# A four-layer graph network on one core: norm and projection in one stage, batch norm in blocks, part tables on ScalarE, scatter landings waited for later

## The reference, cut to what matters

```
deg_isqrt = max(segment_sum(1, dst), 1) ** -0.5
x = layernorm(x + gat_gat(x))                 # layer 0: two attention convolutions, relu between
x = layernorm(x + conv_conv_conv(x))          # layer 1: 3x elu(segment_sum(x[src]) @ W_rel + b + x @ W_root)
x = layernorm(x + batch_layer(x, deg_isqrt))  # layer 2
x = layernorm(x + attention(x, edge_attr))    # layer 3

attention: h = x @ W (4 heads of 64), a_src = h . att_src, a_dst = h . att_dst per head
           e = leaky_relu(a_src[src] + a_dst[dst]); softmax of e over the edges of each dst
           out[dst] += h[src] * softmax (times edge_attr in layer 3)
batch_layer: y = segment_sum(edge_weight * x[src]) + eps_weight * x
             h = relu(batchnorm(y @ w1.T));  y = (h @ w2.T) * deg_isqrt
             return relu(batchnorm(y)) + x      # batch norm: mean and variance over the nodes
```

## Time and profile before

| what | value |
|---|---|
| time, median of 3 runs | 8349.84 us (8339.62 to 8362.3) |
| the profiled execution's own time | 8344.37 us |
| its span in the trace | 8342.6 us |
| PE busy | 4909.4 us, 59% of the span |
| VectorE busy | 3812.1 us, 46% |
| ScalarE busy | 1028.3 us, 12% |
| POOL busy | 5501.9 us, 66% |
| granted clock of TensorE, mean | 0.783 of full speed |

### The profile page before, as it was taken

The page is one execution under the profiler, slowest core; times in us unless marked ns, Lnnn a source line. Parts: engine busy times, 40 slices in busy tenths (PEclk is TensorE's granted clock), DMA queues, the critical chain, the costliest instruction groups (busy, mean ns, idle before and its releaser), DMA issues. The chain is left out here.

```text
span 8342.6 us, 83489 instructions
## 1 busy us (share of the span) xinstructions
PE 4909.4 (59%) x17596; PEld 3782.0 (45%) x17597; DVE 3812.1 (46%) x6764; ACT 1028.3 (12%) x2857; POOL 5501.9 (66%) x5858
## 2 busy tenths in 40 slices
PE   4455565555562666666666666666566666455554
PEld 3344444344452554555545555455444453344443
DVE  5566665566665222242222422225222236566666
ACT  2000003000003000020000200003333323000003
POOL 5777754777733777757777577775777750777770
PEclk7677777787786887888877888788677787777776
DMA  5444433444424443344433444334333334444441
GB/s 177 133 119 117 117 84 109 118 119 117 117 60 151 133 132 105 105 139 133 134 105 105 136 133 135 106 105 145 109 105 105 105 96 134 130 119 119 119 118 65
DMA packets 499012, 982.41 MB, mean 118 GB/s; under 512 B 121598, under 2 KB 303930, under 8 KB 498177
## 3 DMA queue, kind: packets, MB, share of 16 engines
q0 software_dynamic: 274784, 746.53, 32.0%
q1 hardware_dynamic: 155901, 176.58, 6.7%
q10 hardware_dynamic: 68080, 56.84, 2.1%
HBM read 889.06 MB, written 97.65 MB: 118 GB/s over the span
## 5 line engine op out<-in xcount | busy, mean ns | idle before, releaser
L1578 POOL DMA_INDIRECT l1aa_messages<-table,l1aa_index x784 | 741.1, 945 | 465.0 <-issue 238.5
L1578 POOL DMA_INDIRECT l2a_messages<-table,l2a_index x784 | 741.2, 945 | 259.0 <-issue 238.5
L1578 POOL DMA_INDIRECT l1ca_messages<-table,l1ca_index x784 | 741.2, 945 | 249.4 <-issue 238.5
L1578 POOL DMA_INDIRECT l1ba_messages<-table,l1ba_index x784 | 741.2, 945 | 248.9 <-issue 238.5
L1205 POOL DMA_INDIRECT l3a_messages<-table_h,l3a_index x782 | 745.1, 953 | 238.2 <-issue 237.0
L1205 POOL DMA_INDIRECT l0aa_messages<-table_h,l0aa_index x782 | 743.4, 951 | 238.2 <-issue 238.2
L1205 POOL DMA_INDIRECT l0ba_messages<-table_h,l0ba_index x782 | 743.2, 950 | 238.2 <-issue 238.2
L1742 PE MATMUL l1aa_sums<-l1aa_messages,l1aa_member 128*128 x1952 | 584.4, 461 | 457.1 <-SPq L1587 449.4
L1742 PE MATMUL l2a_sums<-l2a_messages,l2a_member 128*128 x1952 | 612.5, 484 | 400.5 <-ACT l2a_messages L1626 396.7
L1742 PE MATMUL l1ba_sums<-l1ba_messages,l1ba_member 128*128 x1952 | 584.6, 462 | 364.0 <-SPq L1587 359.5
L1742 PE MATMUL l1ca_sums<-l1ca_messages,l1ca_member 128*128 x1952 | 585.3, 462 | 362.1 <-SPq L1587 358.2
(11 more groups left out here) (649 smaller groups left out, 6998.7 us busy)
## 6 DMA issues: line engine op xcount, KB each, us to landing
table<-l_acc SPq DMA_DIRECT2D x10, 1280.0 KB
l2b_xin<-table SPq DMA_DIRECT2D x100, 128.0 KB, 2.0
l1aa_messages<-table,l1aa_index POOLq DMA_INDIRECT x784, 2.8
l1ba_messages<-table,l1ba_index POOLq DMA_INDIRECT x784, 2.7
l1ca_messages<-table,l1ca_index POOLq DMA_INDIRECT x784, 2.8
l2a_messages<-table,l2a_index POOLq DMA_INDIRECT x784, 2.7
l0aa_messages<-table_h,l0aa_index POOLq DMA_INDIRECT x782, 3.0
l0ba_messages<-table_h,l0ba_index POOLq DMA_INDIRECT x782, 2.9
```

Source lines behind the costliest of these rows:

```text
L1578: pool.indirect_dma_start(out=ring4[:, g % ROUND, j, 0:D], out_offset=None, in_=table, in_offset=bass.IndirectOffsetOnAxis(ap=index[:, g * ...
```

## The change

It has five parts.

1. `started` becomes a semaphore of the whole program, `k.started`, which is never cleared. The waits for it at the end of the prelude, of l0e and of the projection before layer 3 are gone. The attend phase gets an argument `starts` (1, 2 or 3), and SP issues index, same and local, then waits for `starts * 16 * NT`, and only then loads `start_dram`.
2. In the prelude the order on TensorE becomes project(17, 25), turn_place(1), turn_at(1), project(25, 35), local table of the sums, project(35, 50), local table of attention.
3. In the joins 24 activations of ScalarE (Copy with `of_pair`'s column as scale) make the member tables, four of them ahead of the exponential; TensorE waits for each part's table as it comes to it.
4. l2b: the first stage goes by blocks of four tiles. The product with w1 is made for 512 columns at once, ScalarE copies it to `zT`, VectorE takes statistics of 512 columns, and only 13 of them are aggregated. In the last stage the relu runs in place on `zT` by blocks, and TensorE turns `zT` directly. The slots of x are eight, the loops are written out, the four columns are loaded from ScalarE's queue, TensorE begins on the weights alone, and n_norm is stored and loaded after the load of tile 16.
5. l2n and l3p become one phase `norm_project_phase`, named l3p. ScalarE norms each tile in `acc` (Identity with scale and bias), TensorE turns it from there, nothing is loaded again. The normed table is stored in ten stores of 640 KB that stand between the stores of h on SP. `h_out` has eight slots and `h_ps` four.

```diff
-            pool.wait_ge(started, 16 * NT)
...
-            project(17, 22)
+            project(17, 25)
             turn_place(1)
             turn_at(1)
-            project(22, 30)
+            project(25, 35)
             step_local_on_tensor(pe, k, ws, wide[2])
-            project(30, NTP)
+            project(35, NTP)
             step_local_on_tensor(pe, k, wa, wide[2])
...
-            sp.dma_start(start, start_dram[0:ELEM].rearrange("(r e) h -> r (e h)", e=RL)).then_inc(starts_in, 16)
             sp.dma_start(same, same_dram).then_inc(starts_in, 16)
             sp.dma_start(local[:], steps.local_dram).then_inc(local_in, 16)
+            sp.wait_ge(k.started, starts * 16 * NT)
+            sp.dma_start(start, start_dram[0:ELEM].rearrange("(r e) h -> r (e h)", e=RL)).then_inc(starts_in, 16)
...
+            def members(a, b):
+                for n in range(a, b):
+                    act.activation(member[W, n, :], one_hot[W], ACT.Copy, scale=of_pair[W, n:n + 1]).then_inc(member_made, 1)
+
+            act.wait_ge(hot_made, 1)
+            members(0, 4)
             act.wait_ge(less_made, 1)
             act.activation(weight[W], weight[W], ACT.Exp).then_inc(weight_made, 1)
+            members(4, NCUT)
 
...
-            pe.wait_ge(member_made, 1)
+            pe.wait_ge(parts_made, 1)
             for n in range(NCUT):
+                pe.wait_ge(member_made, n + 1)
...
-            st(dve.tensor_tensor(member[W], repeat_outer(one_hot[W], NCUT), repeat_inner(of_pair[W], P), ALU.mult))
...
+            def store_x(n):
+                sp.wait_ge(normed, (n + 1) * LOAD)
+                rows = table_out[n * LOAD * P:(n + 1) * LOAD * P, :].rearrange("(t p) d -> p t d", p=P)
+                sp.dma_start(rows, acc3[:, n * LOAD:(n + 1) * LOAD, 0:D]).then_inc(x_stored, 16)
+
+            for t in range(NTP):
+                if t % LOAD == 0:
+                    store_x(t // LOAD)
+                sp.wait_ge(h_made, t + 1)
+                sp.dma_start(table_h[t * P:(t + 1) * P, :], h_out[:, t % 8, :]).then_inc(stored[t % 8], 16)
...
+            act.wait_ge(norm_ready, 1)
+            for i in range(NTP + BEHIND):
+                if i < NTP:
+                    here = acc3[:, i, 0:D]
+                    act.activation(here, here, ACT.Identity, scale=var[:, i:i + 1], bias=mean[:, i:i + 1]).then_inc(normed, 1)
+                t = i - BEHIND
+                if t >= 0:
+                    act.wait_ge(turned, t + 1)
+                    if t >= 2:
+                        act.wait_ge(summed, t - 1)
+                    act.copy(xt[:, t % 2, :], xt_ps[t % 2][:, 0:D]).then_inc(xt_made, 1)
+
+        @block.tensor
+        def _(pe):
+            def turn(t):
+                pe.wait_ge(normed, t + 1)
+                if t >= 2:
+                    pe.wait_ge(xt_made, t - 1)
+                for c in range(2):
+                    at = t * MSGW + c * P
+                    ins = pe.transpose(xt_ps[t % 2][:, c * P:(c + 1) * P], acc[:, at:at + P], k.ident[:])
+                ins.then_inc(turned, 1)
+
+            def multiply(t):
+                pe.wait_ge(xt_made, t + 1)
+                if t >= 4:
+                    pe.wait_ge(h_made, t - 3)
+                for c in range(2):
+                    ins = pe.matmul(h_ps[t % 4][:, 0:WE], xt[:, t % 2, c * P:(c + 1) * P], w_sb[:, c, :],
+                                    start=(c == 0), stop=(c == 1))
+                ins.then_inc(summed, 1)
+
...
+            dve.sem_inc(norm_ready, 1)
+            dve.wait_ge(w_in, 64)
+            weights_with_scores(dve, st, w_sb, att, prod)
+            dve.sem_inc(w_ready, 1)
+            for t in range(NTP):
+                dve.wait_ge(summed, t + 1)
+                if t >= 8:
+                    dve.wait_ge(stored[t % 8], t // 8 * 16)
+                dve.tensor_copy(k.att[:, t * 2 * H:(t + 1) * 2 * H], h_ps[t % 4][:, D:WE])
+                dve.tensor_copy(h_out[:, t % 8, :], h_ps[t % 4][:, 0:WE]).then_inc(h_made, 1)
...
+            sp.dma_start(eps_w[:], eps_weight.partition_broadcast(P)).then_inc(eps_in, 16)
+
+            def load(t, sem):
+                sp.dma_start(xin[:, t % SLOTS, :], table_in[t * P:(t + 1) * P, :]).then_inc(sem[t % SLOTS], 16)
+
+            for t in range(NTP):
+                if t >= SLOTS:
+                    sp.wait_ge(y_made, t - SLOTS + 1)
+                load(t, loaded)
+                if t == 2 * SLOTS:
+                    sp.wait_ge(degT_made, 1)
+                    sp.dma_start(norm_dram.rearrange("(t p) -> t p", p=P), degT[0:NTP, :]).then_inc(deg_stored, 16)
+                    sp.wait_ge(deg_stored, 16)
+                    sp.dma_start(n_norm[:], norm_dram.partition_broadcast(P)).then_inc(norm_in, 16)
+            for t in range(NTP):
+                if t < SLOTS:
+                    sp.wait_ge(y_made, t + (NTP - 1 - t) // SLOTS * SLOTS + 1)
...
-            pe.wait_ge(small_in, 144)
+            pe.wait_ge(w_in, 64)
...
+            def turn(t):
                 pe.wait_ge(y_made, t + 1)
+                if t >= 2:
                     pe.wait_ge(yT_made, t - 1)
                 for c in range(2):
+                    ins = pe.transpose(ps[4 + t % 2][:, c * P:(c + 1) * P], yin[:, t % 4, c * P:(c + 1) * P], k.ident[:])
                 ins.then_inc(turned, 1)
 
+            def multiply(n):
+                b, w = blocks[n]
+                pe.wait_ge(yT_made, (b + w) // P)
+                if n >= 2:
+                    pe.wait_ge(z_made, n - 1)
                 for o in range(2):
                     for c in range(2):
+                        ins = pe.matmul(ps[2 * (n % 2) + o][:, 0:w], wT[:, 0, c, o * P:(o + 1) * P],
+                                        yT[:, n % 2, c, 0:w], start=(c == 0), stop=(c == 1))
                 ins.then_inc(summed, 1)
 
+            for t in range(NTP):
+                turn(t)
+                if t >= 2 and (t - 2) % BT == BT - 1:
+                    multiply((t - 2) // BT)
+            multiply(len(blocks) - 1)
+            pe.wait_ge(z_made, len(blocks))
...
+            def take(t):
+                n, j = t // BT, t % BT
                 act.wait_ge(turned, t + 1)
+                if n >= 2:
+                    act.wait_ge(summed, n - 1)
+                act.copy(yT[:, n % 2, :, j * P:(j + 1) * P],
+                         ps[4 + t % 2][:, 0:D].rearrange("p (c n) -> p c n", c=2)).then_inc(yT_made, 1)
+
+            def keep(n):
+                b, w = blocks[n]
+                act.wait_ge(summed, n + 1)
+                for o in range(2):
+                    ins = act.copy(zT[:, o, b:b + w], ps[2 * (n % 2) + o][:, 0:w])
+                ins.then_inc(z_made, 1)
+
+            for t in range(NTP):
+                take(t)
+                if t >= 4 and (t - 4) % BT == BT - 1:
+                    keep((t - 4) // BT)
+            for n in range((NTP - 4) // BT, len(blocks)):
+                keep(n)
 
...
+            for b, w in blocks:
                 for o in range(2):
+                    ins = act.activation(zT[:, o, b:b + w], zT[:, o, b:b + w], ACT.Relu,
                                          bias=bias[:, o:o + 1], scale=scale[:, o:o + 1])
...
+            def add_own(t):
+                dve.wait_ge(loaded[t % SLOTS], (t // SLOTS + 1) * 16)
+                if t >= 4:
+                    dve.wait_ge(turned, t - 3)
+                dve.scalar_tensor_tensor(yin[:, t % 4, :], xin[:, t % SLOTS, :], eps_w[:], acc3[:, t, 0:D],
                                          op0=ALU.mult, op1=ALU.add).then_inc(y_made, 1)
 
+            def block_stat(n, stats):
+                b, w = blocks[n]
+                for o in range(2):
+                    dve.bn_stats(stats[:, o, n * 6:(n + 1) * 6], zT[:, o, b:min(b + w, N)]).then_inc(stats_made, 1)
+
+            for t in range(NTP):
+                add_own(t)
+                if t >= 7 and (t - 7) % BT == BT - 1:
+                    n = (t - 7) // BT
+                    dve.wait_ge(z_made, n + 1)
+                    block_stat(n, block_stats[0])
+            for n in range((NTP - 7) // BT, len(blocks)):
+                dve.wait_ge(z_made, n + 1)
+                block_stat(n, block_stats[0])
+            dve.wait_ge(stats_made, 2 * len(blocks))
+            dve.wait_ge(cols_in, 64)
```

330 lines of the change are left out of this document (96 added, 234 removed).

## The result

The changed kernel takes 8265.67 us (median of 4 runs, 8262.86 to 8277.6); the kernel before, on the same chip, 8347.40 (median of 4, 8339.62 to 8362.3). The ratio is 0.9907 with a 95% interval of 0.9895 to 0.9919, so 68 to 88 us faster. Predicted were 8268 and 8240 to 8304.

The account below looks back on a forecast made before the run. POOL's gathers fill the attend and sum phases and move as blocks, so only the chains between them gain: 3.0 + 7 + 8.7 + 21 + 37.6 = 77.3 off 8344.4 gives 8267, plus 1: 8268 us, range 8240 to 8304.

Parts of the forecast that it names:

- The reading of the chain: Whole kernel: gathers on POOL move as blocks; a microsecond saved in the chains between them is saved at the end.
- The start load behind the landing: Start of attend phases: the load comes at worst some 2 us later, within VectorE's slack; costed at nothing.
- Landing: Phase boundaries behind l0e and l3p: dropping the wait for scatters to land saves 1.5 us each, 3.0 together.
- rival B: Boundaries behind scatters: the silent microseconds all stay and the landing lies under them; 4.5 us less gain, 8273; chance 0.13.
- Prelude: End of the prelude: reordered projection ends 5 us earlier, the dropped landing wait saves 2; together 7.
- Joins: Three joins: member tables moved from VectorE to ScalarE save 2.9 us each, exponential 0.5 late; 8.7 together.
- l2b: Batch norm layer: start 2.5, first stage 8, aggregate 2, second stage -0.5, last stage 9; gain 21 us.
- Fused phase: Norm and projection as one, before layer 3: POOL's scatters pace it; gain 37.6 us, bounds 28 and 40.
- A: Boundaries behind scatters: the silent microseconds go with the wait, 11 us more gain, 8257; chance 0.14.
- C: l2b's first stage: PE runs dry behind VectorE's statistics, up to 34 us, or the n_norm load starves xin; 8302; chance 0.07.
- E: Attend tails: PE's clock falls to 0.50, costing 121 us in three tails; 8388, slower than before; chance 0.02.
- D: Fused phase: x stores between h stores on SP make VectorE wait for slots, 31 us; 8299; chance 0.07.

Follow-up runs that it names:

- gap_late: The changed kernel without the last 24 of l3p's 49 scatters, and with n_norm loaded after stage one's loads: 8261.5 us, ratio 0.9896 to the kernel before.
- again: The changed kernel run once more, unaltered, in another group of runs: 8269.2 us against 8348.5 for the kernel before, ratio 0.9906.
- p39_slots4: The changed kernel with four more tiles projected ahead of the prelude's local table and four h_out slots in the fused phase: 8264.8 us, ratio 0.9901.
- u_wait: The changed kernel with the landing waits back at the ends of the prelude, l0e and l3p, on a slow chip: 10432.7 us, ratio 0.9936.
- wait_again: The changed kernel with the same three landing waits back, on another slow chip: 10444.7 us, ratio 0.9919 to the kernel before.

## Why the prediction was right

- **The reading of the chain** held: gathers move as blocks, and what was saved between them arrived, but for the 3 to 4 us by which the prelude and l0e vary from trace to trace. The gains outside the gathers sum to 85 and 76 in two traces, and the times moved by 82 and 79; 77.3 were predicted. The start load behind the landing, costed at nothing, cost nothing: the first softmax step stands 46.5 to 47.5 behind the first gather in before and 46.9 to 47.6 in after.
- **Landing**: 1.5 taken at two boundaries and 2 at the prelude's, 1.3 to 1.9 measured at all three. The argument, that the silent part comes after all traffic and so isn't landing, is shown by the two wait runs, and gap_late shows whose it is. The Trainium skill's fixed cost of about 2.0 per DMA ("DMA: Bandwidth & Descriptors", "Anatomy of one DMA — SWDGE (gpsimd) path") gave the upper side of it. Two sums beside this term slipped: with 2 for the prelude, rival B is 5.0 less and not 4.5, and the page's price would add 1.0 and not 1.5.
- **Prelude**: 7 predicted, 6.5 measured in after (2.2 in again, late from before the edit), with the right size by luck. The prediction had PE's idle of 4.44 ahead of the local table shrink. On the quick chips it stayed (5.0), since VectorE has the table's operands some 16.5 us after the turn in either order; what counts is how many tiles are projected before it. Five more were, and 5 x 1.1 is the gain. What the edit did gain of idle time stood at the turn of places: 1.68 in before, none in after. That 5 us were still left ahead of the table was not seen, and p39_slots4 took them.
- **Joins**: 2.9 each predicted, 3.1 measured from the first turn to the first product; of this 2.3 and 2.8 arrive in the stretches of the last two joins, where the work behind the first product takes 0.4 to 0.5 longer. The half microsecond for a late exponential was not there; the activations take 0.30 and not 0.45 each. The Trainium skill's price ("ScalarE: Activation LUTs", "What ACT_TABLE_LOAD costs"), 0.29 each and 3.3 per join, was nearer than the row of 482 ns, which has two pointer operands and 128 partitions.
- **l2b**: 21 predicted, 24.5 measured. Start 2.5 and 2.6, first stage 8 and 9.1, aggregate 2.0 and 1.9. The half microsecond taken for n_norm was not lost (gap_late); the second stage came out 0.6 longer in after for no reason that is known, 49.7 against 49.1 from its first relu to its last statistics. The last stage has 9 and 11.7 (47.3 to 35.6 from its first relu to the last row statistics; the window of before in the earlier trace rows leaves out its first 0.65). It is the mis-sized term: I took VectorE's busy time of before, 36.0, as its floor. VectorE's timeline in after shows why it is less:

```profile
6987.34 0.40 DVE L2725 SCALAR_TENSOR_TENSOR l_acc<-l2b_xin,l2b_ps 128x256 f32<-128x256 f32 x1
6987.66 0.42 DVE L2729 BATCH_NORM_STATS2 k_row_stats<-l_acc 128x6 f32<-128x256 f32 x1
6988.00 0.40 DVE L2725 SCALAR_TENSOR_TENSOR l_acc<-l2b_xin,l2b_ps 128x256 f32<-128x256 f32 x1
```

  Each lasts 0.40 to 0.42 and the next starts after 0.32 to 0.34, so the 100 take 33.2 when none waits; behind a wait the one ahead counts with its full length.
- **Fused phase**: 37.6 predicted, 39.7 and 38.4 measured on quick chips and 38.2 between two traces of a slow one. The first scatter came 11.3 after the start, not 12.5, the pace was POOL's.
- **Rivals.** A and B were bracketed, C did not appear (a block takes 4.89, under 5.5), E did not: the clock of the tail is 1.00. D did not on quick chips. On slow ones the fused phase is longer, 86.3 instead of 73.1 in u_wait, and one line of its waits looks like D:

```profile
DVE k_att L2246 <- DMA l2b_xin<-table: 14.0, 7, 2.4
```

  The name of the tensor is the profile's guess, and the line can wait for a slot of h_out. But it does so only from the ninth tile on, and the first of these waits is at the eighth, in VectorE's timeline:

```profile
8695.52 0.42 DVE L2247 COPY l3p_h_out<-l3p_h_ps 128x264 f32<-128x264 f32 x1
8698.33 0.17 DVE L2246 COPY k_att<-l3p_h_ps 128x8 f32<-128x8 f32 x1 [2.38 <-DMA l2b_xin<-table]
```

  TensorE's product for this tile had ended at 8695.75. At the same place ScalarE starts a copy (L2194, at 8696.89) 2.0 us after TensorE's turn for it had ended, with nothing left to wait for, and TensorE then waits for that copy. Such stops of VectorE return every few tiles, in wait_again too. So this first stop is no wait for a slot. D's mechanism is not shown by any run, and what stops the engines on these chips is open; the expectations that speak of slow stores or of late gathers had taken such waits for late transfers. Yet u_wait and wait_again, which lack some 4 us of the change, are 72 and 81 us faster than before there: both forms of the stage are slowed alike.

## What to carry to other kernels

Between two blocks that nothing touches, sum by stretches: the parts add up, and one trace per part settles what five runs of a total can't. Count a part from an instruction just ahead of the edit, and look at a second trace of the same kernel: here the prelude and l0e moved by 3 to 4 us between two of them. For an engine that will no longer wait, take the spacing of its instructions back to back as the floor, not its busy time in a stage where it waited. Where PE idles ahead of work that another engine paces, the question is not whether the idle time shrinks but how much independent work has been put in front of it.

## What the hardware showed that was not expected

- Two kinds of chips: in three of the five groups of runs the kernel before ran in 10441 to 10539 us instead of 8340 to 8362. The page of u_wait on one of them:

```profile
L1205 POOL DMA_INDIRECT l3a_messages<-table_h,l3a_index x782 | 745.8, 954 | 694.4 <-SPq L1244 462.9
L1587 POOL DMA_INDIRECT l1aa_messages<-table,l1aa_index x784 | 743.3, 948 | 641.1 <-DMA l1aa_index<-src_dram 241.8
```

The gathers take the same 954 ns, but 463 us of POOL's idle time end by SP freeing slots (next to none in the earlier trace rows), and of l1aa's 641 us of idle time 242 end by the load of an index. The pages of the profile show no slower transfers: the packets of POOL's queue took 25.6% of the span of 10436.9 us in u_wait and 33.0% of 8275.9 in after, 2672 and 2731 us, for the same 746.53 MB. What holds the engines up there was not tried.
- POOL's next instruction comes 5.6 us behind the last scatter of a phase, with hardly any traffic (2 GB/s in the first microsecond, 0 behind it, in after); l2b, which ends without scatters, costs 0.9. What POOL does in it stays open. In the prelude it is 10.7. There the last local table is still stored (issued at 189.31, traffic until 192), and then some 6 us pass in which nothing shows; why so long stays open too.
- The length of POOL's gathers differs between executions of one kernel by 0.3% (945 and 948 ns), which is 18 us of this program. The profiled execution of after, with the longer ones, is 11 to 15 us slower than the other three, of which no profile exists.
